# First stage of a two-layer kernel: GpSimd's fills behind the normalizations, the lambda chain ahead of the rows, weights split as q, k, v

## The chip, the cores and the metric

The kernel runs on one core of a Trainium2 chip. The metric is the device time of one execution in microseconds, from three timed runs of the kernel before; the median counts. The profile is of one execution, taken on its own.

## The reference

Two layers are computed, each an attention followed by a feed-forward part, each part added to the running rows `x`. Only the first attention is touched, and of it only the part up to q, k and v:

```python
def _layernorm(x, axis=-1, eps=1e-05):
    return (x - mean(x)) / sqrt(var(x) + eps)

x = L0_attn_x                       # (2, 1024, 256) float32
h = _layernorm(x)
qkv = h @ W_attn                    # (256, 768): q1, k1, q2, k2 (128 columns each), v (256)
lam = exp(dot(lambda_q1, lambda_k1)) - exp(dot(lambda_q2, lambda_k2)) + LAMBDA_INIT
attn1 = einsum('bthd,bshd->bhts', q1, k1) * scale
attn2 = einsum('bthd,bshd->bhts', q2, k2) * scale
score = softmax(attn1 - lam * attn2)          # 16 heads, hd = 8
out = (1 - LAMBDA_INIT) * einsum('bhts,bshd->bthd', score, v)
x = x + out @ W_proj
```

After it come a feed-forward part with ternary weights that keeps the largest tenth of its hidden units, a linear attention with 32 heads and a routed feed-forward part.

## The kernel before

The kernel is written as stages, each a block of five engine programs that wait for each other on semaphores only; a stage ends at a barrier of all engines, after which SyncE (SP) clears its semaphores. The order of each engine's work is written out by hand. The first stage is `stage_qkv` (line 158).

The 2048 rows are worked off in four chunks of 512 (`d.NC` = 4), each four tiles of 128 rows (`d.TPC`), with E = 256 as two halves of 128 (`d.KT` = 2). The rows stay in the tensor `residual` (X). For each chunk c:

- VectorE: `normal(c)` takes the statistics of the four tiles (lines 110, 113, 115: the variance plus epsilon), waits for ScalarE's root (line 137, `norm_root`), refines its reciprocal (lines 121 to 125) and applies mean and scale (line 142, one TENSOR_SCALAR for each tile, into `xn`).
- TensorE: `turn(c)` (line 366) transposes the eight 128 x 128 blocks of `xn` into PSUM.
- Each value that goes into a product is split in a high part and a low part; `mm_split` (line 153) makes three products of them. ScalarE copies out the high part (`high`, line 324), VectorE subtracts it (`low`, line 268).
- TensorE: four groups of 6 products of 512 columns for q and k (`ps_q`), then `turn(c + 1)`, then two times 12 products of 256 columns for v (`ps_v`).
- ScalarE and VectorE split q and k again (line 345, and `low_qk`, lines 277 and 282), and SP writes both parts to a DRAM tensor, two transfers for each of the four groups. ScalarE copies v into `v_rows` (`vall`, line 354), 32 columns for each head, of which 16 are v.

When chunk 1 (the last of the first batch) has been written, SP loads the first stack of q and k back from DRAM, into `qst` and `kst` of ring place 0; the attention stage needs it at its start.

Once, before all this: GpSimd makes the identity, fills `v_rows` with zeros (line 244, 128 x 8192), its column 16 of each head with a constant (line 245), and rows of the three `kst` tensors with ones (line 249, six fills of 32 x 2048). The weights are split into `w_hi` (ScalarE, lines 331 and 332) and `w_lo` (VectorE, lines 297 and 298), for each half k all of q, k and v, behind the normalization of chunk 0. The four lambda vectors come as rows of one partition (line 218, SP's queue); VectorE multiplies and sums them (lines 290, 291), ScalarE takes exp (line 335; Exp and Sqrt lie in different activation tables, so each switch is an ACT_TABLE_LOAD), VectorE makes the row of scales of it (lines 302 to 306), and TensorE turns this row into a column (line 373), which VectorE copies to `qs`. The scale `qs` is needed when q leaves PSUM. TensorE's q and k products of chunk 0 stand behind the column and behind the last `w_lo`.

The kernel already uses products whose result nobody reads: line 660 in the attention stage, 128 x 512 in full precision.

Of the kernel before, what the change touches and what calls it, by code (L numbers as in the profile page):

```python
# [28 lines left out]
def as_f32(ap):  # L29
    return ap.bitcast(F32)  # L30
# [127 lines left out]
def stage_qkv(nc, d, io, keep, scratch):  # L158


    with ExitStack() as ctx:
# [15 lines left out]
        lam_in = xn[0:1, 1]  # L177
        lam_pr = st.sb("lam_pr", [1, 2, d.E])
# [12 lines left out]
        dots, exps, row_ok, col_ok, qs_ok = (st.sem(n) for n in ("dots", "exps", "row_ok", "col_ok", "qs_ok"))  # L191
# [3 lines left out]
        v_ps, v_ok, v_init, pad_ok = (st.sem(n) for n in ("v_ps", "v_ok", "v_init", "pad_ok"))  # L195
# [12 lines left out]
        with nc.Block() as block:  # L208
            @block.sync
            def _(sp):  # L210
                for c in range(d.NC):
                    sl = slice(c * d.TPC, (c + 1) * d.TPC)
                    sp.dma_start(X[:, sl, :], x_tiles[:, sl, :]).then_inc(x_in[c], 16)
                    if c == 0:
                        sp.dma_start(w_raw[:], io["L0_attn_W_attn"].rearrange("(k p) n -> p k n", p=P))\
                            .then_inc(w_in, 16)
                        for n, name in enumerate(("q1", "k1", "q2", "k2")):
                            sp.dma_start(lam_in[:, n, :],
                                         io["L0_attn_lambda_" + name].rearrange("(a e) -> a e", a=1))\
                                .then_inc(lam_s, 16)  # L220
                for c in range(d.NC):
# [7 lines left out]
                    if c == d.S // d.CH - 1:  # L229
                        sp.wait_ge(pad_ok, 2 * len(kst))  # L230
# [6 lines left out]
            def _(pool):  # L237
# [6 lines left out]
                link(nc.gpsimd.memset(vall[:], 0.0))  # L244
                nc.gpsimd.memset(vall[:, :, :, d.HD:d.HD + 1], 1.0 / (1.0 - LAMBDA_INIT)).then_inc(v_init, 1)
                pool.wait_ge(v_init, 1)
                for i in range(2 * len(kst)):
                    rows = slice(ROW2 * (i % 2) + 32, ROW2 * (i % 2) + 64)
                    nc.gpsimd.memset(as_f32(kst[i // 2][rows, :, :]), 1.0).then_inc(pad_ok, 1)
                    pool.wait_ge(pad_ok, i + 1)  # L250

            @block.vector
            def _(dve):
                link = chain(dve, dv)

                def normal(c):
                    dve.wait_ge(x_in[c], 16)
                    norm_stats(nc, dve, link, w[c % 2], [X[:, d.TPC * c + j, :] for j in range(d.TPC)], c // 2 + 1)
# [25 lines left out]

                nc.vector.memset(one[:], 1.0)
                link(nc.vector.memset(row[:], 1.0))
                normal(0)

                dve.wait_ge(lam_s, 64)
                link(nc.vector.tensor_tensor(lam_pr[:], lam_in[:, 0::2, :], lam_in[:, 1::2, :], ALU.mult))  # L290
                nc.vector.reduce_sum(lam[0:1, 0:2], lam_pr[:], AX.X).then_inc(dots, 1)
                for k in range(d.KT):
                    dve.wait_ge(w_hi_ok, k + 1)
                    for part in range(2):
                        src, hi, lo = halves(k, part)
                        for a in range(2):
                            nc.vector.tensor_tensor(lo[:, :, a], src[:, :, a], as_f32(hi)[:, :, a], ALU.subtract)
                    nc.vector.tensor_tensor(w_lo[:, k, 2 * d.E:], w_raw[:, k, 2 * d.E:], as_f32(w_hi[:, k, 2 * d.E:]),
                                            ALU.subtract).then_inc(w_lo_ok, 1)
                low(0)  # L300
                dve.wait_ge(exps, 1)
                link(nc.vector.tensor_tensor(lam[0:1, 4:5], lam[0:1, 2:3], lam[0:1, 3:4], ALU.subtract))
                link(nc.vector.tensor_scalar(lam[0:1, 5:6], lam[0:1, 4:5], LAMBDA_INIT, -scale, ALU.add, ALU.mult))
                r = row[0:1, :].rearrange("p (h a e) -> p a h e", a=2, e=HD2)
# [5 lines left out]
                for c in range(d.NC):  # L310
                    if c + 1 < d.NC:
                        normal(c + 1)
# [2190 lines left out]
```

## Time and profile before

| what | value |
|---|---|
| median of three runs | 1221.81 us (1221.64 to 1226.63) |
| span of the profiled execution | 1222.5 us, 0.7 above the median |
| TensorE (PE) busy in the span | 1090.1 us (89%) |
| VectorE (DVE) busy | 916.0 us (75%) |
| ScalarE (ACT) busy | 623.8 us (51%) |
| GpSimd (POOL) busy | 218.6 us (18%) |
| end of the first stage (first instruction of the second) | 64.20 us |

The trace names each instruction by engine, line of the kernel, operation, output and inputs, with start and duration. PEld is TensorE's weight load, which overlaps products. A row "x4" is four instructions merged, and its duration runs from the first start to the last end. What stands in brackets is the idle time of the engine before the instruction, and who ended it. The names carry the stage: `qkv_xn` is `xn`, `residual` is X, `att_out` holds the high parts of q and k.

### The profile page before, as it was taken

Reading aid. Unit: us, or ns where it says so; the run is one execution under the profiler, and the core shown is the slowest. Engines: PE = TensorE matmul, PEld = TensorE weight load, DVE = VectorE, ACT = ScalarE, POOL = GpSimd, SP = SyncE. Lnnn points to the kernel's source line nnn. Section 1 sums busy time; section 2 is a strip of 40 time slices with the busy share of each in tenths; the row PEclk is TensorE's granted clock in tenths of the full one; section 3 lists DMA queues with packets and bytes.
Section 4 is the critical chain, followed back from the end, with each engine's and each line's share of the span. In section 5 each row is a group of like instructions: output and inputs, shape, how many; then the busy total and the mean of one; then the engine's idle time right before and its main releaser. Section 6 shows DMA issues by size and latency. Waiting matters only on the chain. (4 is left out here: it accounts for less than half of the span.)

```text
span 1222.5 us, 18399 instructions
## 1 busy us (share of the span) xinstructions
PE 1090.1 (89%) x7034; PEld 752.9 (62%) x7034; DVE 916.0 (75%) x1702; ACT 623.8 (51%) x1092; POOL 218.6 (18%) x173
## 2 busy tenths in 40 slices
PE   2969999999999998877877989999996999999978
PEld 2823333333333346666666768888885889899866
DVE  7778999999999824488898886555553878897832
ACT  2525878878788763766641233333334333433323
POOL 6004500000000001000034203000001744744300
PEclk9959999999999999888988989999997899999989
DMA  2880232143030000000000021011001000000010
GB/s 95 198 258 18 37 54 39 16 54 53 2 54 2 2 1 31 1 1 0 1 18 1 1 91 35 18 35 35 18 1 61 2 1 1 1 1 1 1 66 5
DMA packets 24850, 40.02 MB, mean 33 GB/s; under 512 B 3116, under 2 KB 12344, under 8 KB 24760
## 3 DMA queue, kind: packets, MB, share of 16 engines
q1 hardware_dynamic: 24760, 38.82, 13.7%
q8 instruction: 56, 0.92, 0.3%
q14 instruction: 34, 0.28, 0.1%
HBM read 28.06 MB, written 10.49 MB: 32 GB/s over the span
## 5 line engine op out<-in xcount | busy, mean ns | idle before, releaser
L721 DVE TENSOR_REDUCE att_mx<-att_ps_m 128x2 f32<-128x1024 f32 x256 | 310.9, 1225 | 25.1 <-PE att_ps_m L587 21.5
L698 ACT ACTIVATE att_prob<-att_ps_s 128x512 f32<-128x512 f32 x512 | 278.2, 596 | 89.9 <-PE att_ps_s L637 77.9
L653 PE MATMUL att_ps_o<-att_prob,v_rows 128*32 128x256 f32 (+1 forms) x1920 | 159.4, 405 | 0.0
L1931 POOL TENSOR_TENSOR qry_prod<-qry_qr,lin_ksum 128x512 f32<-128x512 f32 x64 | 92.9, 1452 | 303.0 <-ACT qry_qr L2052 288.9
L637 PE MATMUL att_ps_s<-qst,kst 50*128 50x512 f32 x512 | 128.0, 496 | 11.0 <-ACT att_prob L698 10.4
L637 PEld LDWEIGHTS att_ps_s<-qst,kst 50*128 50x128 f32 x512 | 48.1, 183 | 123.7 <-ACT att_prob L698 114.2
L587 PE MATMUL att_ps_m<-kst,qst 48*128 48x512 f32 x512 | 110.6, 427 | 9.0 <-DVE att_mx L721 6.9
L2052 ACT ACTIVATE qry_qr<-qry_ps_q 128x512 f32<-128x512 f32 x64 | 38.3, 598 | 132.9 <-PE qry_ps_q L153 124.0
L153 PE MATMUL qry_ps_o<-qry_m,qry_n_hi 128*128 128x256 f32 x512 | 99.7, 293 | 0.4 <-DVE qry_n_lo L1961 0.3
L1642 DVE SCALAR_TENSOR_TENSOR key_k_lo<-kf_ps,key_k_hi 128x512 fp32r<-128x512 f32 x64 | 44.2, 691 | 61.6 <-ACT key_k_hi L1720 61.0
L653 PEld LDWEIGHTS att_ps_o<-att_prob,v_rows 128*32 128x32 f32 x1920 | 38.1, 108 | 84.7 <-ACT att_prob L698 71.1
L153 PEld LDWEIGHTS qry_ps_o<-qry_m,qry_n_hi 128*128 128x128 f32 x512 | 78.6, 191 | 1.3 <-issue 0.7
L153 PE MATMUL qry_ps_o<-qry_m,qry_n_lo 128*128 128x256 f32 x256 | 71.8, 281 | 0.0
L1720 ACT ACTIVATE key_k_hi<-kf_ps 128x512 fp32r<-128x512 f32 x64 | 38.1, 597 | 64.3 <-PE kf_ps L153 57.1
L587 PEld LDWEIGHTS att_ps_m<-kst,qst 48*128 48x128 f32 x512 | 50.8, 194 | 23.5 <-DVE att_mx L721 19.8
L1961 DVE TENSOR_TENSOR qry_n_lo<-qry_ps_t,qry_n_hi 128x512 fp32r<-128x512 f32 x64 | 44.3, 692 | 23.2 <-ACT qry_n_hi L2041 21.4
L1951 DVE SCALAR_TENSOR_TENSOR qry_qn<-qry_rec,qry_qr 128x512 f32<-128x512 f32 x64 | 56.3, 880 | 2.2
L915 POOL MEMSET mlp_ones<- 128x128 f32 x1 | 0.2, 209 | 322.9 <-POOLq L525 322.9
L1946 DVE TENSOR_REDUCE qry_nrm<-qry_prod 128x8 f32<-128x512 f32 x64 | 43.7, 683 | 9.1 <-POOL qry_prod L1931 7.0
L153 PE MATMUL kf_ps<-key_k_hi,kf_xk 128*128 128x512 f32 x128 | 46.5, 404 | 4.6 <-DVE key_k_lo L1642 4.6
L153 PE MATMUL qry_ps_q<-qry_w_hi,kf_xt 128*128 128x512 f32 x128 | 47.4, 414 | 3.3 <-DVE qry_w_lo L2010 3.3
L153 PEld LDWEIGHTS qry_ps_o<-qry_m,qry_n_lo 128*128 128x128 f32 x256 | 48.9, 191 | 0.0
(425 smaller groups left out, 2336.8 us busy)
## 6 DMA issues: line engine op xcount, KB each, us to landing
qst<-qk_parts SPq DMA_DIRECT2D x48, 128.0 KB, 4.7
kst<-qk_parts SPq DMA_DIRECT2D x48, 128.0 KB, 7.3
qk_parts<-att_out SPq DMA_DIRECT2D x16, 256.0 KB, 5.6
qk_parts<-qk_lo SPq DMA_DIRECT2D x16, 256.0 KB, 5.8
residual<-L_attn_x SPq DMA_DIRECT2D x4, 512.0 KB, 6.1
lin_wq_raw<-L_attn_Wv SPq DMA_DIRECT2D x4, 512.0 KB, 3.7
lin_wq_raw<-L_attn_Wq SPq DMA_DIRECT2D x4, 512.0 KB, 5.3
lin_wq_raw<-L_attn_Wo SPq DMA_DIRECT2D x4, 512.0 KB, 3.9
```

The costliest lines, as they stand in the source:

```text
L153: ins = nc.tensor.matmul(out, a, b, start=first and n == 0, stop=last and n == len(terms) - 1)
L587: ins = nc.tensor.matmul(ps_m[:, n % 2, r, :], qst[g % RING][rows, v % NB, j, t * P:(t + 1) * P], kst[g % RING][rows, j, half * d.CH:(half ...
L637: ins = nc.tensor.matmul(ps_s[:, (n + r) % BANKS, :], kst[g % RING][rows, j, s * P:(s + 1) * P], qst[g % RING][rows, t, j, :], start=True, ...
L653: ins = nc.tensor.matmul(ps_o[32 * h:32 * h + 32, cols], vall[:, NS * b + s, h0 + h, :], prob[:, u % PR, h, cols], start=s == 0, stop=s == ...
L698: nc.scalar.activation(prob[:, u % PR, 2 * j + r, :], ps_s[:, (n + r) % BANKS, :], ACT.Exp).then_inc(exp_ok, 1)
L721: nc.vector.reduce_max(mx[:, v % 2, :, m], ps_m[:, n % 2], AX.X).then_inc(m_rd, 1)
L1642: nc.vector.scalar_tensor_tensor(out=k_lo[:, i % 2, :], in0=ps_k[:, i % 2, :], scalar=0.0, in1=as_f32(k_hi[:, i % 2, :]), op0=ALU.max, op1 ...
L1931: nc.gpsimd.tensor_tensor(prod[:, u % 2, :], qr[:, u % 2, :], ksum[:, b, cols(n)], ALU.mult).then_inc(pr_ok, 1)
L1946: link(nc.vector.tensor_reduce(nrm[:], prod[:, u % 2, :].rearrange("p (h e) -> p h e", e=HW), AX.X, ALU.add))
L1951: nc.vector.scalar_tensor_tensor(out=qn[:, u % 2, :].rearrange("p (h e) -> p h e", e=HW), in0=rec[:].unsqueeze(2).to_broadcast([P, HPB, HW ...
L1961: nc.vector.tensor_tensor(n_lo[:, u % 2, :], ps_t[:, u % 2, :], as_f32(n_hi[:, u % 2, :]), ALU.subtract).then_inc(n_ok, 1)
L2052: nc.scalar.activation(qr[:, u % 2, :], ps_q[:, u % 2, :], ACT.Relu).then_inc(q_ok, 1)
```

## The change

GpSimd. Of its fills only the two of `kst` 0 stay in front; then it does the scalar tail of lambda (two operations on one element and one on 64), waits until all four chunks are normalized, and does the other fills: column 16 of each head, the columns behind it (15 of 32, where before it zeroed all 32), and `kst` 1 and 2. SP's wait ahead of the first stack load is for `kst` 0 alone. ScalarE's wait for the fill of `v_rows` goes.

Lambda. The four vectors are loaded by ScalarE's queue, as 128 partitions x 2 elements each. TensorE makes the two dots as four products of one column, ScalarE takes exp of them straight from PSUM, ahead of its first root. The row of scales is prepared by VectorE as constants.

Weights. Split part by part (0: q of both kinds, 1: k, 2: v) rather than half by half; TensorE's q products wait for part 0, its k products for part 1, v for part 2, and each half k of chunk 0 for its own `xt_lo`. VectorE does low_w(0), low(0), low_w(1), the statistics of chunk 1, low_w(2), and then waits for the column.

TensorE. Unread products of 128 columns: six after the identity, sixteen after the dots, four after the column. In chunk 0 the order is q and k, first half of v, `turn(1)`, second half of v.

The diff, with unchanged lines mostly left out and eight spaces of indentation removed:

```diff
 qk_hi = keep["AO"][:].bitcast(F32R).rearrange("p (c j a) e -> p c j (a e)", c=2, j=NQ)
-lam_in = xn[0:1, 1]
-lam_pr = st.sb("lam_pr", [1, 2, d.E])
+lam_in = st.sb("lam_in", [P, 4, d.KT])
 lam = st.sb("lam", [1, 8])
...
 dv, gp, w_hi_ok, w_lo_ok = st.sem("dv"), st.sem("gp"), st.sem("w_hi_ok"), st.sem("w_lo_ok")
-dots, exps, row_ok, col_ok, qs_ok = (st.sem(n) for n in ("dots", "exps", "row_ok", "col_ok", "qs_ok"))
+dots, exps, row_1, row_ok, col_ok, qs_ok = (
+    st.sem(n) for n in ("dots", "exps", "row_1", "row_ok", "col_ok", "qs_ok"))
+WARM = 16
 xn_ok, xt_ps, hi_ok, lo_ok = (st.sem(n) for n in ("xn_ok", "xt_ps", "hi_ok", "lo_ok"))
...
 qk_out = scratch["qk_out"]
-v_ps, v_ok, v_init, pad_ok = (st.sem(n) for n in ("v_ps", "v_ok", "v_init", "pad_ok"))
+v_ps, v_ok, pad_ok = (st.sem(n) for n in ("v_ps", "v_ok", "pad_ok"))
 id_ok, stack_in = st.sem("id_ok"), st.sem("stack_in")
...
                     .then_inc(w_in, 16)
-                for n, name in enumerate(("q1", "k1", "q2", "k2")):
-                    sp.dma_start(lam_in[:, n, :],
-                                 io["L0_attn_lambda_" + name].rearrange("(a e) -> a e", a=1))\
-                        .then_inc(lam_s, 16)
         for c in range(d.NC):
...
             if c == d.S // d.CH - 1:
-                sp.wait_ge(pad_ok, 2 * len(kst))
+                sp.wait_ge(pad_ok, 2)
                 for i in range(d.S // d.CH):
...
-        link(nc.gpsimd.memset(vall[:], 0.0))
-        nc.gpsimd.memset(vall[:, :, :, d.HD:d.HD + 1], 1.0 / (1.0 - LAMBDA_INIT)).then_inc(v_init, 1)
-        pool.wait_ge(v_init, 1)
-        for i in range(2 * len(kst)):
-            rows = slice(ROW2 * (i % 2) + 32, ROW2 * (i % 2) + 64)
-            nc.gpsimd.memset(as_f32(kst[i // 2][rows, :, :]), 1.0).then_inc(pad_ok, 1)
-            pool.wait_ge(pad_ok, i + 1)
+        def pads(i):
+            for r in range(2):
+                rows = slice(ROW2 * r + 32, ROW2 * r + 64)
+                nc.gpsimd.memset(as_f32(kst[i][rows, :, :]), 1.0).then_inc(pad_ok, 1)
+                pool.wait_ge(pad_ok, 2 * i + r + 1)
+        pads(0)
+        pool.wait_ge(exps, 1)
+        link(nc.gpsimd.tensor_tensor(lam[0:1, 4:5], lam[0:1, 2:3], lam[0:1, 3:4], ALU.subtract))
+        link(nc.gpsimd.tensor_scalar(lam[0:1, 5:6], lam[0:1, 4:5], LAMBDA_INIT, -scale, ALU.add, ALU.mult))
+        pool.wait_ge(row_1, 1)
+        r = row[0:1, :].rearrange("p (h a e) -> p a h e", a=2, e=HD2)
+        nc.gpsimd.tensor_scalar(r[:, 1], r[:, 1], lam[0:1, 5:6], None, ALU.mult).then_inc(row_ok, 1)
+        pool.wait_ge(xn_ok, d.NC)
+        link(nc.gpsimd.memset(vall[:, :, :, d.HD:d.HD + 1], 1.0 / (1.0 - LAMBDA_INIT)))
+        link(nc.gpsimd.memset(vall[:, :, :, d.HD + 1:], 0.0))
+        for i in range(1, len(kst)):
+            pads(i)
...
+        def var(c):
+            dve.wait_ge(x_in[c], 16)
+            norm_var(nc, link, w[c % 2], [X[:, d.TPC * c + j, :] for j in range(d.TPC)])
         def normal(c):
-            dve.wait_ge(x_in[c], 16)
-            norm_stats(nc, dve, link, w[c % 2], [X[:, d.TPC * c + j, :] for j in range(d.TPC)], c // 2 + 1)
+            norm_rstd(nc, dve, link, w[c % 2], c // 2 + 1)
             if c >= 2:
...
+        def low_w(part):
+            for k in range(d.KT):
+                dve.wait_ge(w_hi_ok, d.KT * part + k + 1)
+                if part == 2:
+                    ins = nc.vector.tensor_tensor(w_lo[:, k, 2 * d.E:], w_raw[:, k, 2 * d.E:],
+                                                  as_f32(w_hi[:, k, 2 * d.E:]), ALU.subtract)
+                else:
+                    src, hi, lo = halves(k, part)
+                    for a in range(2):
+                        ins = nc.vector.tensor_tensor(lo[:, :, a], src[:, :, a], as_f32(hi)[:, :, a],
+                                                      ALU.subtract)
+            ins.then_inc(w_lo_ok, 1)
         nc.vector.memset(one[:], 1.0)
-        link(nc.vector.memset(row[:], 1.0))
+        r = row[0:1, :].rearrange("p (h a e) -> p a h e", a=2, e=HD2)
+        nc.vector.memset(r[:, 1], 1.0)
+        nc.vector.memset(r[:, 0], scale).then_inc(row_1, 1)
+        var(0)
         normal(0)
-        dve.wait_ge(lam_s, 64)
-        link(nc.vector.tensor_tensor(lam_pr[:], lam_in[:, 0::2, :], lam_in[:, 1::2, :], ALU.mult))
-        nc.vector.reduce_sum(lam[0:1, 0:2], lam_pr[:], AX.X).then_inc(dots, 1)
-        for k in range(d.KT):
-            dve.wait_ge(w_hi_ok, k + 1)
-            for part in range(2):
-                src, hi, lo = halves(k, part)
-                for a in range(2):
-                    nc.vector.tensor_tensor(lo[:, :, a], src[:, :, a], as_f32(hi)[:, :, a], ALU.subtract)
-            nc.vector.tensor_tensor(w_lo[:, k, 2 * d.E:], w_raw[:, k, 2 * d.E:], as_f32(w_hi[:, k, 2 * d.E:]),
-                                    ALU.subtract).then_inc(w_lo_ok, 1)
+        low_w(0)
         low(0)
-        dve.wait_ge(exps, 1)
-        link(nc.vector.tensor_tensor(lam[0:1, 4:5], lam[0:1, 2:3], lam[0:1, 3:4], ALU.subtract))
-        link(nc.vector.tensor_scalar(lam[0:1, 5:6], lam[0:1, 4:5], LAMBDA_INIT, -scale, ALU.add, ALU.mult))
-        r = row[0:1, :].rearrange("p (h a e) -> p a h e", a=2, e=HD2)
-        nc.vector.tensor_scalar(r[:, 1], r[:, 1], lam[0:1, 5:6], None, ALU.mult)
-        nc.vector.tensor_scalar(r[:, 0], r[:, 0], scale, None, ALU.mult).then_inc(row_ok, 1)
+        low_w(1)
+        var(1)
+        low_w(2)
         dve.wait_ge(col_ok, 1)
         nc.vector.tensor_copy(qs[:, 0:1], ps_v[:, 0, 0, 0:1]).then_inc(qs_ok, 1)
-        dve.wait_ge(qs_ok, 1)
         for c in range(d.NC):
             if c + 1 < d.NC:
+                if c:
+                    var(c + 1)
                 normal(c + 1)
+            if c == 0:
+                dve.wait_ge(qs_ok, 1)
             low_qk(c)
...
+        def high_w(part):
+            for k in range(d.KT):
+                if part == 2:
+                    ins = nc.scalar.activation(w_hi[:, k, 2 * d.E:], w_raw[:, k, 2 * d.E:], ACT.Copy)
+                else:
+                    src, hi, _ = halves(k, part)
+                    ins = nc.scalar.activation(hi, src, ACT.Copy)
+                ins.then_inc(w_hi_ok, 1)
+        for n, name in enumerate(("q1", "k1", "q2", "k2")):
+            nc.scalar.dma_start(lam_in[:, n, :], io["L0_attn_lambda_" + name].rearrange("(p k) -> p k", p=P))\
+                .then_inc(lam_s, 16)
+        act.wait_ge(dots, 1)
+        nc.scalar.activation(lam[0:1, 2:4], ps_v[0:1, 1, 1, 0:2], ACT.Exp).then_inc(exps, 1)
         norm_root(nc, act, w[0], 1)
         act.wait_ge(w_in, 16)
-        for k in range(d.KT):
-            for part in range(2):
-                src, hi, _ = halves(k, part)
-                nc.scalar.activation(hi, src, ACT.Copy)
-            nc.scalar.activation(w_hi[:, k, 2 * d.E:], w_raw[:, k, 2 * d.E:], ACT.Copy).then_inc(w_hi_ok, 1)
+        for part in range(3):
+            high_w(part)
         high(0)
-        act.wait_ge(dots, 1)
-        nc.scalar.activation(lam[0:1, 2:4], lam[0:1, 0:2], ACT.Exp).then_inc(exps, 1)
         for c in range(d.NC):
...
                 act.wait_ge(v_ps, 2 * c + j + 1)
-                if c == 0:
-                    act.wait_ge(v_init, 1)
                 t = d.TPC * c + 2 * j
...
+        def keep_busy(n):
+            for _ in range(n):
+                nc.tensor.matmul(ps_q[:, NQ - 1, 0:P], ident[:], ident[:], start=True, stop=True)
+        def values(c, j):
+            if c == 0:
+                pe.wait_ge(qs_ok, 1)
+                pe.wait_ge(w_lo_ok, 3)
+            else:
+                pe.wait_ge(v_ok, 2 * (c - 1) + j + 1)
+            for i in range(2):
+                t = slice((2 * j + i) * P, (2 * j + i + 1) * P)
+                for k in range(d.KT):
+                    ins = mm_split(nc, ps_v[:, j, i, :], xt_hi[:, c % 2, k, t], xt_lo[:, c % 2, k, t],
+                                   w_hi[:, k, 2 * d.E:], w_lo[:, k, 2 * d.E:], k == 0, k == d.KT - 1)
+            ins.then_inc(v_ps, 1)
         pe.wait_ge(id_ok, 1)
+        keep_busy(6)
+        pe.wait_ge(lam_s, 64)
+        for n in range(2):
+            for k in range(d.KT):
+                ins = nc.tensor.matmul(ps_v[0:1, 1, 1, n:n + 1], lam_in[:, 2 * n, k:k + 1],
+                                       lam_in[:, 2 * n + 1, k:k + 1], start=k == 0, stop=k == d.KT - 1)
+        ins.then_inc(dots, 1)
+        keep_busy(WARM)
         turn(0)
...
             .then_inc(col_ok, 1)
-        pe.wait_ge(w_lo_ok, d.KT)
+        keep_busy(4)
         for c in range(d.NC):
-            pe.wait_ge(lo_ok, d.KT * (c + 1))
             for j in range(NQ):
...
                     pe.wait_ge(qk_lo_ok, NQ * (c - 1) + j + 1)
+                elif j % 2 == 0:
+                    pe.wait_ge(w_lo_ok, j // 2 + 1)
                 for k in range(d.KT):
+                    if j == 0:
+                        pe.wait_ge(lo_ok, d.KT * c + k + 1)
                     cols = slice(j * P, (j + 1) * P)
...
                 ins.then_inc(qk_ps, 1)
+            if c == 0:
+                values(c, 0)
+                turn(c + 1)
+                values(c, 1)
+                continue
             if c + 1 < d.NC:
...
             for j in range(2):
-                if c == 0:
-                    pe.wait_ge(qs_ok, 1)
-                else:
-                    pe.wait_ge(v_ok, 2 * (c - 1) + j + 1)
-                for i in range(2):
-                    t = slice((2 * j + i) * P, (2 * j + i + 1) * P)
-                    for k in range(d.KT):
-                        ins = mm_split(nc, ps_v[:, j, i, :], xt_hi[:, c % 2, k, t], xt_lo[:, c % 2, k, t],
-                                       w_hi[:, k, 2 * d.E:], w_lo[:, k, 2 * d.E:], k == 0, k == d.KT - 1)
-                ins.then_inc(v_ps, 1)
+                values(c, j)
 st.clear()
```

## Rows read from the trace of the kernel before

**Rows 1.** The page's first line: span and number of instructions.

```profile
span 1222.5 us, 18399 instructions
```

**Rows 2.** Stretches (us, busy and count by engine, PEclk, DMA share, GB/s).

```profile
0.00:24.54 24.54, 2.45 (x10) 2.06 (x10) 18.26 (x38) 7.29 (x13) 19.09 (x14) 1.00 0.37 118
...
35.46:44.80 9.34, 9.34 (x60) 8.33 (x59) 8.10 (x26) 4.95 (x9) 0.00 (x0) 1.00 0.59 218
```

**Rows 3.** Timeline, 0 to 20 us, all engines (start, us, engine, line, work, [idle <-releaser]).

```profile
1.53 6.92 POOL L244 MEMSET v_rows<- 128x8192 f32 x1
...
5.32 1.41 DVE L110 BATCH_NORM_STATS2 qkv_stats<-residual 128x6 f32<-128x256 f32 x4 [4.30 <-DMA residual<-L_attn_x]
...
8.51 0.53 POOL L245 MEMSET v_rows<- 128x256 f32 x1
...
8.62 0.71 ACT L331 ACTIVATE qkv_w_hi<-qkv_w_raw 128x256 fp32r<-128x256 f32 x2
...
9.10 11.22 POOL L249 MEMSET kst<- 32x2048 f32 x6
...
11.16 7.42 DVE L142 TENSOR_SCALAR qkv_xn<-residual,qkv_mv,qkv_rstd 128x256 f32<-128x256 f32 x4
...
18.50 0.67 DVE L290 TENSOR_TENSOR qkv_lam_pr<-qkv_xn 1x512 f32<-1x512 f32 x1
```

**Rows 4.** Single lines, 0 to 60 us (duration ns min/median/max, first and last start).

```profile
L142 DVE TENSOR_SCALAR qkv_xn<-residual,qkv_mv,qkv_rstd x16: 404/410/1972, 11.2 to 47.9; 128x256 f32<-128x256 f32 x16
...
L115 DVE TENSOR_SCALAR qkv_ve<-qkv_mv x4: 170/170/1301, 7.2 to 45.5; 128x4 f32<-128x4 f32 x4
...
L124 DVE TENSOR_SCALAR qkv_t<-qkv_t x4: 170/170/1572, 9.4 to 46.6; 128x4 f32<-128x4 f32 x4
```

**Rows 5.** Timeline, 20 to 36.6 us.

```profile
20.95 0.88 DVE L297 TENSOR_TENSOR qkv_w_lo<-qkv_w_raw,qkv_w_hi 128x128 fp32r<-128x128 f32 x4
...
22.83 1.28 ACT L137 ACT_TABLE_LOAD   x1
...
24.03 0.58 PE L373 MATMUL qkv_ps_v<-qkv_one,qkv_row 1*128 1x1 f32 x2 [3.37 <-DVE qkv_row L306]
...
24.84 1.41 DVE L110 BATCH_NORM_STATS2 qkv_stats<-residual 128x6 f32<-128x256 f32 x4
...
25.13 0.63 PE L153 MATMUL qkv_ps_q<-qkv_xt_lo,qkv_w_hi 128*128 128x512 f32 x1
...
27.14 0.18 DVE L121 RECIPROCAL qkv_r<-qkv_sd 128x4 f32<-128x4 f32 x1 [0.27 <-ACT qkv_sd L137]
...
28.12 0.45 PE L153 MATMUL qkv_ps_q<-qkv_xt_hi,qkv_w_lo 128*128 128x512 f32 x1
...
28.15 1.38 DVE L142 TENSOR_SCALAR qkv_xn<-residual,qkv_mv,qkv_rstd 128x256 f32<-128x256 f32 x4
...
29.45 1.41 DVE L277 SCALAR_TENSOR_TENSOR qk_lo<-qkv_ps_q,qkv_qs,att_out 128x512 fp32r<-128x512 f32 x2
...
31.82 1.03 PE L366 MATMUL qkv_ps_t<-ident,qkv_xn 128*128 128x128 f32 x8
...
33.25 1.28 DVE L268 TENSOR_TENSOR qkv_xt_lo<-qkv_ps_t,qkv_xt_hi 128x512 fp32r<-128x512 f32 x2
...
35.56 0.40 PE L153 MATMUL qkv_ps_q<-qkv_xt_hi,qkv_w_hi 128*128 128x512 f32 x1
...
35.79 0.40 PE L153 MATMUL qkv_ps_q<-qkv_xt_lo,qkv_w_hi 128*128 128x512 f32 x1
```

**Rows 6.** Timeline of TensorE, second stage, unread products (line 660).

```profile
86.47 2.07 PE L660 MATMUL att_ps_s<-v_rows,att_ones 128*128 128x512 f32 x2
...
93.96 1.12 PE L660 MATMUL att_ps_s<-v_rows,att_ones 128*128 128x512 f32 x2
```

**Rows 7.** Timeline of ScalarE, end of the first stage.

```profile
62.54 0.60 ACT L354 ACTIVATE v_rows<-qkv_ps_v 128x512 f32<-128x512 f32 x1 [0.84 <-PE qkv_ps_v L153]
```

**Rows 8.** DMA queues, 6 to 10 us (packets, MB, share of 16 engines).

```profile
q1 hardware_dynamic: 1345, 1.44, 107.6%
```

## The prediction

> **What bounds the kernel now.** I read the page first. One core runs stages that follow each other behind barriers, over a span of 1222.5 us [rows 1]; that profiled execution is 0.7 us above the median of the timed runs, 1221.8, so a saving read from the trace is taken off the median unchanged. The change touches the first stage alone, so the question is how much earlier the second stage can begin. The table of stretches [rows 2] says where to look. In the first 24.54 us TensorE is busy for 2.45 us and VectorE for 18.26: this is a start-up chain. In a steady chunk (35.46 to 44.80) TensorE is busy throughout and VectorE for 8.10 of 9.34 us: TensorE sets the pace there. The change can gain in the start-up and cannot shorten a steady chunk. I measure everything by one mark, the first product of chunk 1, at 35.56 [rows 5]; after it the stage is the same code, apart from GpSimd's fills.
>
> **What the start-up waits for.** The timeline [rows 3] shows VectorE sitting until the first rows land at 5.32. The normalization of chunk 0 then ends at 18.58. Chunk 1 does the same work from 24.84 to 29.53, in 4.7 us [rows 5]. The groups by line say where the difference lies: the apply (L142) has a median of 0.410 us and a maximum of 1.972, and two four-element operations (L115, L124) have 0.170 and maxima of 1.301 and 1.572 [rows 4]. These long ones all stand beside GpSimd's fills (v_rows from 1.53, kst from 9.10, six in 11.22 us, so 1.87 us each), and the four applies end about where fills end: 7.42 us for four is one per fill of 1.87. The excess is 1.13 + 1.40 + 6.04 = 8.6 us. Not every VectorE operation suffers: the statistics beside the fills take 1.41 us for four, as they do alone in chunk 1, and a TENSOR_TENSOR at 18.50 runs inside a fill in 0.67 us, for 512 elements of one partition. So what is slow is TENSOR_SCALAR from SBUF to SBUF beside a GpSimd fill.
>
> **The change, part by part.**
>
> *GpSimd's fills.* Only the two fills of kst 0 stay in front (2 x 1.87 from about 1.5, over at about 5.3, when the rows land). VectorE's TENSOR_SCALARs then run clear of fills: -8.6 us on the path. The rest goes behind the last normalization, whose last apply starts at 47.9 and ends at 48.3 in the old clock [rows 4]: 0.53 for the strided ones, 15/32 of 6.92 = 3.2 for the zeros, 4 x 1.87 = 7.5, in all 11.3, so to 59.6, when ScalarE's last copy starts at 62.54 and ends at 63.1 [rows 7]. Nothing waits inside: 0 on the path. If the zeros cost per element what the strided fill does (0.53 / 256 = 2.07 ns, 3840 elements, 7.9 us) it ends at 64.3, 1.2 us late; 0 to 1.2, I take 0, since only a fixed cost in the short fill need explain its rate. Beside these fills VectorE runs subtractions out of PSUM. No row has such a subtraction beside a fill; the nearest is the TENSOR_TENSOR at 18.50, which was not held up. If each of them had to wait for the fill that runs, like the applies, the first would lose up to 3.2 - 0.7 = 2.5 us and the next two 1.87 - 0.7 = 1.2 each, 4.9 in all ahead of chunk 3's products, less the 1 us by which VectorE leads TensorE (34.53 against 35.56); bounds 0 to 3.9, I take 0.
>
> The Trainium skill ("SBUF — State Buffer", section "SBUF: two separate sides") says that VectorE and GpSimd share a port pair as an exclusive lock for a whole instruction, against VectorE operations in a two-port mode or, where GpSimd reads SBUF, with two SBUF inputs. By that rule a fill would leave a subtraction from PSUM alone, and the loss at the end would be 0. No row here shows that pair.
>
> *The four lambda loads.* They leave SP's queue, are issued by ScalarE, and become 128 partitions x 2 elements each: 512 packets of 8 bytes where there were four rows of 1 KB. No row prices an 8-byte packet. In the busiest stretch of the row loads, 1345 packets took 107.6% of 16 engines for 4 us, 51 ns each, nearly all of them 1 KB [rows 8]. Below: 0 (they move in the gaps before the rows come). Above: 32 packets per engine x 51 ns = 1.6 us, added to the first rows. I take 0.8: rows at 6.1. Lambda is taken to land with them at 6.1.
>
> The Trainium skill ("DMA: Bandwidth & Descriptors", section "Specifications") puts full rate at 512 bytes or more and says that smaller transfers are done as read-modify-write. That speaks against this edit; what it would do if it were expensive is the third rival.
>
> *The lambda chain.* It was TENSOR_TENSOR, a reduction, an Exp between two table loads (1.28 each [rows 5]), four small VectorE operations, a product and a copy, with the qkv products standing behind it. Now the dots are products on TensorE (0.6 us for a product with its second pass, [rows 5], so 6.1 to 6.7), Exp 0.2, and the table load for Sqrt 1.3: ScalarE is ready for the root at about 8.3. The variance is ready at 6.1 + 2.0 = 8.1. So the root comes 0.2 late, and the rows are normalized at 6.1 + 4.7 + 0.2 = 11.0, where it was 18.6. GpSimd takes the scalar tail in its idle time. Behind Exp on ScalarE stand the root, six weight copies (two in 0.71, so 2.1 us, to about 10.7 [rows 3]) and the copy of the turned rows, which comes later.
>
> *Unread products.* Six before lambda, sixteen after it, four after the turn. They stand in TensorE's queue ahead of the turn. A full-precision product appears as two records, 2.07 us for 512 columns while TensorE ran at the lower of its two levels (1.2 GHz) and 1.12 at the upper (2.4) [rows 6]; a quarter, for 128 columns, is 0.52 and 0.28. From 6.7, sixteen take 4.5 us (to 11.2) or 8.3 (to 15.0). In the start-up the granted clock is printed as 1.00 [rows 2], yet the durations tell of the lower level first: TensorE was at work from 24.03 to 28.12, and then its products fell from 0.63 to 0.45 us and less [rows 5]. By that, eight at 0.52 and eight at 0.28 end at 13.1; if the clock has risen sooner, after the six early ones, sooner. I take the turn at 12.0, between 11.2 and 13.1, so the unread products hold the turn up by about 1 us over the normalized rows. It was at 18.73. What they give back (eight qkv products at 0.63 instead of 0.40) is not on the path that follows.
>
> *Weights split as q, k, v.* From the turn T to the end of low(0): 2.7 us (31.82 to 34.53 in chunk 1). low_w(0) is done by 11.9, so it hides behind ScalarE's copy. Then VectorE carries low_w(1), four TENSOR_TENSORs, 0.9; var(1), 2.0 (24.84 to the end of L115; the reciprocal follows at 27.14, after the root); low_w(2), as many columns as low_w(1) in half the instructions, 0.8; the copy of qs 0.2; the rest of the normalization of chunk 1, 27.14 to 29.53, 2.4; low_qk(0), 4 x 0.7 = 2.8; the first half of low(1), 0.65. Sum 9.75. So chunk 1's first product is at T + 12.45. Is TensorE ready? Turn, one product and four unread ones end at T + 2.4, 24 products started 0.23 apart (35.56 to 35.79) at T + 7.9, the first half of the values, 1.4 (a chunk of 9.3 less 5.5 and the turn's 1.0, halved), at T + 9.3; the second turn waits for normalized rows until T + 9.1, so it ends, 1.0 later and with a little for the handover, at T + 10.4, and the second half of the values at T + 11.8. VectorE decides by 0.6 us. If eight of the 24 products last 0.63 instead of 0.40, as the first ones did here, TensorE is the later one, by 1.2 us.
>
> *Sum.* 12.0 + 12.45 = 24.45 against 35.56: 11.1 us. Of that 6.7 is the earlier turn (8.6 of fills, less what the lambda loads and unread products cost), and 4.4 the shorter way from turn to chunk 1.
>
> *Afterwards.* VectorE now starts on chunk 2's rows 0.65 us after TensorE's mark, where it led by 1.0 us (34.53 against 35.56). It needs 2.3 + 2.4 + 2.8 + 0.65 = 8.15 us to the next low half, so it is there 8.8 us after the mark, against a TensorE chunk of 9.3: in time, with 0.5 to spare. SP's writes to DRAM and the stack loads hang on chunks 0 and 1 and move along. So 1221.8 - 11.1 = 1210.7.
>
> **The rivals.**
>
> 1. *Unread products end early.* The turn goes with the normalized rows, undelayed by small packets: T = 10.0 to 11.2, saving 13.1 to 11.9: 1208.7 to 1209.9. For it: only 0.28 each at 2.4 GHz. Chance 0.2.
>
> 2. *They stay at 1.2 GHz, or lambda is late.* T = 13.1 to 15.0, saving 10.0 to 8.1: 1211.8 to 1213.7. For it: the first eight qkv products of the profile, all at the lower level. Chance 0.17.
>
> 3. *Slower: 8-byte packets.* Lambda gates Exp, Exp the root, and the root everything. T = landing + 5.0 by the root or + 6.8 by the unread products. The saving is 23.1 - T, so it is gone with a landing at 16.3 and turns into +0.5% (6.1 us) at 22.4. That takes 0.64 us per packet instead of 0.051, giving 1228. Nothing in the rows excludes it outright. Chance 0.03.
>
> 4. *Given back.* VectorE's lost lead makes each of three chunks wait: 1.5 us each plus a hold by the late fills of 3.9 leaves 11.1 - 8.4 = 2.7: 1219.1. Against it: 8.10 busy of 9.34. Chance 0.06.
>
> 5. *Only the late fills cost*, 1.2 to 3.9: 1211.9 to 1214.6. Chance 0.06.
>
> **How the numbers follow.** My forecast (T from 11.2 to 13.1, 1209.9 to 1211.8) has 0.48. I give 1210.7 and the range 1208.3 to 1214.6, which takes in rivals 1, 2 and 5 with 0.4 us of spread of the runs; 0.09 and some unknown stay outside. 0.5% (6.1 us) is about what this kernel's measurement can tell from no change. Faster by more: 0.48 + 0.2 + 0.17 + 0.06 = 0.91. Within: 0.06. Slower: 0.03.
>
> **What would show it.** The four applies of chunk 0 take 1.4 us, and L115 and L124 0.17. The rows land at 5.3 to 6.9. The first turn stands at 11.2 to 13.1 with TensorE at work right up to it; if a gap stands ahead of it, the normalized rows decide. Chunk 1's first product comes at about 24.5, released by VectorE's low(1), and the later chunks keep 9.2 to 9.4 us. GpSimd's last fill ends about 3 us before the stage does; subtractions beside it keep 0.69. The second stage keeps its length. Wrong would be: a root that waits long for Exp, a fill at the barrier, or later stages whose lengths change by microseconds.

## The result and the profile after

The kernel after runs in 1213.01 us (median of four, 1212.19 to 1216.01) against 1223.14 for the kernel before on the same chip (1221.64 to 1226.63). The ratio is 0.9929 with a 95% interval of 0.9908 to 0.9949: 8.7 us faster, between 6.2 and 11.2. The prediction said 11.1 us faster, 1208.3 to 1214.6. The direction and the range held. The sum was 2.4 us above the measured 8.7; the timed runs alone don't show this, as 11.1 lies inside their interval, but the trace does, with 8.35 us at the end of the stage.

The timeline of the kernel after, 0 to 17 us, all engines:

```profile
1.53 2.93 PE L396 MATMUL qkv_ps_q<-ident 128*128 128x128 f32 x12 [1.53 <-POOL ident L237]
1.53 3.65 POOL L244 MEMSET kst<- 32x2048 f32 x2
...
5.03 1.41 DVE L110 BATCH_NORM_STATS2 qkv_stats<-residual 128x6 f32<-128x256 f32 x4 [4.00 <-DMA residual<-L_attn_x]
...
8.39 0.34 PE L416 MATMUL qkv_ps_v<-qkv_lam_in 128*1 128x1 f32 x8 [3.93 <-DMA qkv_lam_in<-L_attn_lambda_k]
...
8.66 6.35 PE L396 MATMUL qkv_ps_q<-ident 128*128 128x128 f32 x32
8.76 0.16 ACT L355 ACTIVATE qkv_lam<-qkv_ps_v 1x2 f32<-1x2 f32 x1 [4.83 <-PE qkv_ps_v L416]
8.94 1.28 ACT L137 ACT_TABLE_LOAD   x1
...
10.24 0.21 ACT L137 ACTIVATE qkv_sd<-qkv_ve 128x4 f32<-128x4 f32 x1
...
10.47 0.18 DVE L121 RECIPROCAL qkv_r<-qkv_sd 128x4 f32<-128x4 f32 x1 [3.42 <-ACT qkv_sd L137]
...
11.48 1.38 DVE L142 TENSOR_SCALAR qkv_xn<-residual,qkv_mv,qkv_rstd 128x256 f32<-128x256 f32 x4
...
14.84 1.04 PE L389 MATMUL qkv_ps_t<-ident,qkv_xn 128*128 128x128 f32 x8
```

Against [rows 3]: the applies take 1.38 us where they took 7.42. The rows land at 5.03, no later than before. But VectorE's reciprocal waits 3.42 us for ScalarE's root, the root stands behind the table load, that behind Exp, and Exp behind lambda, for which TensorE waited until 8.39. The rows are normalized at 12.86. The turn comes 2 us later still, behind the unread products that end at about 14.8. Both waits are what the change itself put there.

The two lines that tell of GpSimd's fills, single lines of the kernel after (duration ns min/median/max), where [rows 4] had maxima of 1972 and 1301:

```profile
L142 DVE TENSOR_SCALAR qkv_xn<-residual,qkv_mv,qkv_rstd x16: 405/408/414, 11.5 to 39.4; 128x256 f32<-128x256 f32 x16
L115 DVE TENSOR_SCALAR qkv_ve<-qkv_mv x4: 170/171/171, 6.9 to 36.9; 128x4 f32<-128x4 f32 x4
```

The timeline of TensorE gives the marks: chunk 1's first product at 26.42 (35.56 in [rows 5]) and chunk 2's at 35.71. The end of the stage, from the timelines of VectorE, GpSimd, ScalarE and SP's queue:

```profile
39.69 1.41 DVE L288 SCALAR_TENSOR_TENSOR qk_lo<-qkv_ps_q,qkv_qs,att_out 128x512 fp32r<-128x512 f32 x2
39.84 0.60 POOL L255 MEMSET v_rows<- 128x256 f32 x1 [29.77 <-DVE qkv_xn L142]
...
40.50 3.33 POOL L256 MEMSET v_rows<- 128x3840 f32 x1
41.01 0.68 DVE L293 TENSOR_TENSOR qk_lo<-qkv_ps_q,att_out 128x512 fp32r<-128x512 f32 x1
...
43.88 7.38 POOL L244 MEMSET kst<- 32x2048 f32 x4
...
53.47 0.60 ACT L377 ACTIVATE v_rows<-qkv_ps_v 128x512 f32<-128x512 f32 x1 [0.84 <-PE qkv_ps_v L153]
...
54.55 0.46 SPq L224 DMA_DIRECT2D qk_parts<-qk_lo  x1
...
55.85 0.21 POOL L603 MEMSET att_ones<- 128x128 f32 x1 [4.59 <-POOLq L75]
```

GpSimd's fills end at 51.3, 3.7 us ahead of SP's last issue. The subtractions out of PSUM beside them take 0.68, and 1.41 for two, as alone: the hold that the prediction bounded with 3.9 us isn't there. ScalarE is done at 54.07 but SP still issues writes, the last until 55.01, and the second stage starts 0.84 us after that. So the second stage starts 8.35 us sooner (64.20 to 55.85), and not the 9.14 of the mark.

### The profile page after: what moved, and what is told of

Its sections match the earlier page's. It is cut to its first block and busy times, and to the rows that moved or that the text cites. A ratio compares the mean times of both kernels' runs of the same rounds, so it can differ in the third digit from the quotient of the medians.

```text
span 1211.0 us, 18514 instructions
## 1 busy us (share of the span) xinstructions
PE 1093.7 (90%) x7094; PEld 757.6 (63%) x7094; DVE 904.9 (75%) x1697; ACT 621.9 (51%) x1091; POOL 215.8 (18%) x176
```

## The experiments

Each is compared by three times of its own profile: the first turn T, the first product of chunk 1 (the mark), and the start of the second stage; and by the ratio of its time to the kernel before, timed in the same rounds. The kernel before has two profiles, and its mark differs by 0.74 us between them (last row), so a difference of that size at the mark shows nothing.

| kernel | T | mark | second stage | ratio (95%) |
|---|---|---|---|---|
| before | 18.73 | 35.56 | 64.20 | 1 |
| after | 14.84 | 26.42 | 55.85 | 0.9929 (0.9908 to 0.9949) |
| e_fills | 10.16 | 27.19 | 55.7 | 0.9931 (0.9911 to 0.9952) |
| e_nofills | 17.43 | 32.03 | 63.6 | 0.9971 (0.9956 to 0.9987) |
| e_warm0 | 13.26 | 26.93 | 56.5 | 0.9951 (0.9934 to 0.9967) |
| e_root | 13.93 | 25.51 | 54.6 | one run, 1214.51 us |
| e_root_warm0 | 9.92 | 24.30 | 53.9 | 0.9928 (0.9911 to 0.9946) |
| e_rows | 12.41 | 23.99 | 54.0 | one run, 1213.6 us |
| e_merge | 14.26 | 25.84 | 54.5 | 0.9928 (0.9902 to 0.9954) |
| e_best | 9.87 | 22.11 | 50.8 | 0.9880 (0.9858 to 0.9902) |
| e_best_narrow | 9.90 | 23.40 | 53.1 | 0.9882 (0.9865 to 0.9898) |
| e_before_again | 18.73 | 36.30 | 64.5 | one run, 1221.56 us |

**One part alone: the fills.** The kernel before, with only this (and SP's wait for two of the pads, and no v_init):

```diff
-link(nc.gpsimd.memset(vall[:], 0.0))
-nc.gpsimd.memset(vall[:, :, :, d.HD:d.HD + 1], ...)
-for i in range(2 * len(kst)): ...
...
+pads(0)
+pool.wait_ge(xn_ok, d.NC)
+link(nc.gpsimd.memset(vall[:, :, :, d.HD:d.HD + 1], 1.0 / (1.0 - LAMBDA_INIT)))
+link(nc.gpsimd.memset(vall[:, :, :, d.HD + 1:], 0.0))
+for i in range(1, len(kst)):
+    pads(i)
```

> The kernel before with one part of the change: GpSimd's fills moved (only kst 0 in front, the rest behind the fourth normalization). Theory (the fills are the gain): the four applies of chunk 0 take 1.4 us instead of 7.4, the first turn stands at about 10.1 instead of 18.7, the first product of chunk 1 at 35.56 - 8.6 = 27.0, which is within 0.6 us of the full change (26.42), so the time is 8 to 9 us below before and about that of the full change. Rival (lambda, the split of the weights and the unread products carry a third, 4.4 - 0 us as the prediction had it): chunk 1 at 27.0 all the same but at least 3 us of time above the full change.

The first theory held: T 8.57 us sooner, mark 8.37 sooner, and a time that can't be told from that of the full change (0.9931 and 0.9929). Timeline of e_fills:

```profile
8.63 1.38 DVE L142 TENSOR_SCALAR qkv_xn<-residual,qkv_mv,qkv_rstd 128x256 f32<-128x256 f32 x4
...
10.16 1.94 PE L369 MATMUL qkv_ps_t<-ident,qkv_xn 128*128 128x128 f32 x8 [10.16 <-DVE qkv_xn L142]
...
15.47 0.58 PE L376 MATMUL qkv_ps_v<-qkv_one,qkv_row 1*128 1x1 f32 x2 [3.38 <-DVE qkv_row L311]
```

The turn is 4.7 us earlier than in the full change, and 5.3 us then go by before the column: the lambda chain and the weights between turn and products, which the full change removes. All other parts together win 0.8 us at the mark, about the mark's own spread, and nothing at the second stage (55.7 and 55.85).

**All but the fills.** The full change with every fill in front of lambda's tail.

```diff
-pads(0)
+link(nc.gpsimd.memset(vall[:, :, :, d.HD:d.HD + 1], 1.0 / (1.0 - LAMBDA_INIT)))
+link(nc.gpsimd.memset(vall[:, :, :, d.HD + 1:], 0.0))
+for i in range(len(kst)):
+    pads(i)
 pool.wait_ge(exps, 1)
```

> The full change with all of GpSimd's fills back in front (lambda's scalar tail behind them). Theory: the applies of chunk 0 wait for fills again, GpSimd is busy until about 16.5 us and the row of scales comes after it; the first turn goes back to 17 to 19 us and chunk 1 to 29 to 31, so the time is 3 to 5 us above the full change and 5 to 6 below before. Rival (the port matters little once the chain is reordered): chunk 1 at 27 or sooner.

Timeline of VectorE in e_nofills:

```profile
11.41 1.46 DVE L124 TENSOR_SCALAR qkv_t<-qkv_t 128x4 f32<-128x4 f32 x1
...
13.11 4.27 DVE L142 TENSOR_SCALAR qkv_xn<-residual,qkv_mv,qkv_rstd 128x256 f32<-128x256 f32 x4
```

The applies take 4.27 us and L124 1.46 beside the fills; T is 17.43. The mark came at 32.03, 1 us later than expected. The time is about 5 us above the full change, as expected, and 3.5 us below the kernel before, where 5 to 6 were expected. So with the fills in front the other parts are worth 3.5 us, and with the fills moved nothing that the time shows: the two gains don't add up. The second stage's 63.6 says little here: the profiled execution took 1222.93 us, against a median of 1217.72 over twelve, and in it SP issued until 62.76, 3.2 us after ScalarE's last copy, with most of its last sixteen writes at 0.5 to 0.7 us, where the full change has 0.4 to 0.5.

**Without the sixteen unread products.**

```diff
 ins.then_inc(dots, 1)
-keep_busy(WARM)
 turn(0)
```

> The full change without the sixteen unread products after the dots. Theory (they hold the turn): the first turn goes with the normalized rows at 12.9 instead of 14.84, so chunk 1 comes up to 2 us sooner, 24.5 to 25.5, less what a lower clock costs the first qkv products. Rival (they pay for themselves by the clock): the first qkv products take 0.63 instead of 0.40 us and chunk 1 comes no sooner than 26.4.

Timeline of TensorE in e_warm0:

```profile
13.26 1.97 PE L389 MATMUL qkv_ps_t<-ident,qkv_xn 128*128 128x128 f32 x8 [4.19 <-DVE qkv_xn L142]
...
15.67 2.08 PE L396 MATMUL qkv_ps_q<-ident 128*128 128x128 f32 x8
```

T is 1.6 us earlier, but the turn takes 1.97 instead of 1.04 and the four unread products 2.08 instead of 1.16: TensorE is at its lower level there, and the mark is 0.5 us later. The rival held in its size but not in its place: of the 24 qkv products only the first is longer than before (0.68), and the price was paid ahead of them. Where they stand, the sixteen cost a delay and buy back as much. The ratio, 0.9951, is above that of the full change, but the intervals overlap.

**The root ahead of Exp, alone.**

```diff
+norm_root(nc, act, w[0], 1)
 act.wait_ge(dots, 1)
 nc.scalar.activation(lam[0:1, 2:4], ps_v[0:1, 1, 1, 0:2], ACT.Exp).then_inc(exps, 1)
-norm_root(nc, act, w[0], 1)
```

> The full change with ScalarE's first root ahead of Exp and nothing else. Theory (two holds, and the unread products are the outer one): the rows are normalized at 9.8 instead of 12.9, but the sixteen unread products end at 14.8 as before, so the turn and chunk 1 stay within 0.3 us of the full change (14.84, 26.42). Rival (the late root was the hold): the turn at 13 or sooner and chunk 1 at 25 or sooner.

Timeline of VectorE in e_root:

```profile
8.30 1.38 DVE L142 TENSOR_SCALAR qkv_xn<-residual,qkv_mv,qkv_rstd 128x256 f32<-128x256 f32 x4
```

The applies start at 8.30 and end at 9.68, 3.2 us sooner, and the turn still waits for the unread products. They took 5.34 us here (6.35 in the full change), so T and the mark are 0.9 sooner than in the full change, outside the 0.3 expected. The sixteen took 5.3 to 6.4 us in five profiles with the same code: TensorE's level rose 3.5 us after the first of them here and 5.5 us after it in the full change (from 4 or 5 records in half a microsecond to 7).

**Both at once**: the edits of e_root and e_warm0 together.

> As e_warm0, and ScalarE takes its first root ahead of lambda's Exp. Theory (two holds in a row: lambda's landing at 8.39 holds Exp and so the root, the unread products hold the turn): the rows are normalized at 9.7, the turn stands at 9.8, the high parts wait for the weight copies until about 11, and chunk 1 comes at 22.5 to 24.0: 2.5 to 4 us below the full change. Rival (lambda's landing decides anyway, by the scales or by the weight copies behind Exp): chunk 1 at 25 or later, time within 1.5 us of the full change.

T is 9.92 as expected. The mark, 24.30, is 0.3 later than the range: the turn takes 1.97 us again, and the first qkv products after their first take 0.63 us. The stage is 2.0 us shorter than in the full change, less than the 2.5 expected, and in the time (0.9928) nothing of it can be told.

**Lambda as rows.** Loaded as four rows of 1 KB. The dots wait for the rows but read a constant tile, which VectorE fills, so this kernel leaves lambda's value out.

```diff
-nc.scalar.dma_start(lam_in[:, n, :], io["L0_attn_lambda_" + name].rearrange("(p k) -> p k", p=P))
+nc.scalar.dma_start(lam_row[:, n, :], io["L0_attn_lambda_" + name].rearrange("(a e) -> a e", a=1))
```

> The full change with lambda loaded as four rows of 1 KB (4 packets) from ScalarE's queue instead of 512 packets of 8 bytes; the dots read a tile of constants but still wait for the loads, so lambda's value is left out of the computation. Theory (the small packets make lambda late): the dots run by 5.0 to 6.0 instead of 8.39, the root no longer waits (7.1 instead of 10.24), the rows are normalized at 9.7, and the turn follows the unread products, 12 to 12.6. Rival (lambda waits behind the rows and the weights in the DMA engines, whatever its packets): the dots still at 7.5 to 8.5.

Timeline of e_rows, then DMA queues, 0 to 12 us, of the kernel after (packets, MB, share of 16 engines):

```profile
6.43 0.34 PE L418 MATMUL qkv_ps_v<-qkv_lam_in 128*1 128x1 f32 x8 [1.98 <-DMA qkv_lam_row<-L_attn_lambda_k]
...
8.28 0.21 ACT L137 ACTIVATE qkv_sd<-qkv_ve 128x4 f32<-128x4 f32 x1
...
12.41 1.04 PE L391 MATMUL qkv_ps_t<-ident,qkv_xn 128*128 128x128 f32 x8
```

```profile
q1 hardware_dynamic: 2384, 2.88, 70.8%
q10 hardware_dynamic: 576, 0.00, 2.6%
```

The dots run 2.0 us sooner, not the 2.4 to 3.4 expected, and the root still waits (8.28, not 7.1), for Exp and its table load. T is where it was expected. So the form of the load is worth 2 us, and it isn't the engines' time: 576 packets in 2.6% of 16 engines for 12 us are 9 ns each. They land late: the dots start 6.2 us after the last of the four issues, and 4.6 us after it with rows of 1 KB. VectorE starts on the rows at 4.90 here and at 5.03 in the full change, so the small packets hardly delay them. Why they land late isn't shown.

**SP's wide writes.** For chunks 2 and 3 one transfer takes two groups.

```diff
+wide = 2 if c >= d.S // d.CH else 1
-for j in range(NQ):
+for j in range(0, NQ, wide):
-    sp.wait_ge(qk_lo_ok, NQ * c + j + 1)
+    sp.wait_ge(qk_lo_ok, NQ * c + j + wide)
```

> The full change, and SP writes q and k of chunks 2 and 3 with one transfer for two groups instead of one for each (8 issues fewer). In the full change SP's last issue ends at 55.01, 0.94 us after ScalarE's last copy (54.07), and the second stage starts 0.84 after it. Theory (SP's queue ends the stage there): SP is done ahead of ScalarE, the first product of chunk 1 stays at 26.4, and the second stage starts at about 55.0 instead of 55.85. Rival (the barrier waits for ScalarE or for the landing of the stack): the second stage still starts 29.4 us after that product. In the time, 0.85 us is at the edge of what can be told.

The second stage starts 28.65 us after the mark instead of 29.43: 0.8 of the 0.85 expected. SP's last issue still ends after ScalarE's last copy, at 53.67 against 53.49. The mark itself was 0.6 sooner, by shorter unread products (5.62 us). The time doesn't resolve it (0.9928).

**A version made of these findings**: e_root, eighteen unread products ahead of the dots and none behind them, wide writes.

```diff
 pe.wait_ge(id_ok, 1)
-keep_busy(6)
+keep_busy(18)
 pe.wait_ge(lam_s, 64)
...
-keep_busy(WARM)
```

> The full change with ScalarE's first root ahead of Exp, eighteen unread products ahead of the dots in place of six and none of the sixteen behind them, and SP's wide writes of e_merge. Theory: TensorE reaches the upper clock while it waits for lambda (products of 0.49 us each until about 5.5, then 0.26, over at 8.5), the turn stands at 9.9 and takes 1.04, the first qkv product comes at 12.4, chunk 1 at 22.0 to 22.5, the second stage at 50.8 to 51.5, 4.4 to 5 us ahead of the full change; time about 1208.5. Rival (SP's queue or the write of chunk 1 takes the gain away): chunk 1 at 22.0 to 22.5 but the second stage not before 53.

Timeline of e_best:

```profile
1.53 6.88 PE L398 MATMUL qkv_ps_q<-ident 128*128 128x128 f32 x36 [1.53 <-POOL ident L239]
...
8.91 0.34 PE L418 MATMUL qkv_ps_v<-qkv_lam_in 128*1 128x1 f32 x8 [0.50 <-DMA qkv_lam_in<-L_attn_lambda_k]
...
9.87 1.09 PE L391 MATMUL qkv_ps_t<-ident,qkv_xn 128*128 128x128 f32 x8 [0.63 <-DVE qkv_xn L142]
```

The unread products now lie in time in which TensorE waited anyway, and the turn runs at the upper level (1.09) straight behind the normalized rows. Mark and second stage are as expected. By its ratio, 0.9880 (1207.65 us), it is 14.7 us faster than before, between 12 and 17, and its interval lies wholly below that of the full change. The stage is 13.4 us shorter.

**The same with narrow writes**: e_best with SP's loop as it was.

> As e_best, but SP writes q and k of chunks 2 and 3 with one transfer for each group again. Theory (SP's queue ends the stage once TensorE is early): the first product of chunk 1 stays at 22.1 (within 0.7), but the second stage starts 29.7 to 30.5 after it, 52.0 or later, against 28.7 in e_best. Rival (TensorE and ScalarE end the stage): the second stage starts 28.7 after it, at 50.8.

Timelines of TensorE and of ScalarE and GpSimd in e_best_narrow:

```profile
8.55 0.34 PE L416 MATMUL qkv_ps_v<-qkv_lam_in 128*1 128x1 f32 x8 [1.16 <-DMA qkv_lam_in<-L_attn_lambda_k]
9.90 1.09 PE L389 MATMUL qkv_ps_t<-ident,qkv_xn 128*128 128x128 f32 x8 [1.01 <-DVE qkv_xn L142]
...
11.59 2.01 PE L396 MATMUL qkv_ps_q<-ident 128*128 128x128 f32 x8
...
13.83 0.63 PE L153 MATMUL qkv_ps_q<-qkv_xt_lo,qkv_w_hi 128*128 128x512 f32 x1
...
50.37 0.60 ACT L377 ACTIVATE v_rows<-qkv_ps_v 128x512 f32<-128x512 f32 x1 [0.84 <-PE qkv_ps_v L153]
...
53.10 0.21 POOL L602 MEMSET att_ones<- 128x128 f32 x1 [5.05 <-POOLq L75]
```

The second stage starts 29.7 us after the mark, as SP's queue would have it, against 28.7. The mark missed its 22.1 by 1.3 us: TensorE had idled 1.16 and 1.01 us around the dots (0.50 and 0.63 in e_best), and by the four unread products after the column (2.01 us) it was back at the lower level. TensorE's code is the same in both kernels, so this is a difference between two executions, and e_best's mark is the better of the two; how often it comes isn't known. In its time the kernel is as fast as e_best (0.9882), so the wide writes show in the trace, as the 1.0 us between mark and second stage, and not in the time.

**The kernel before, profiled again.**

> The kernel before, unchanged, profiled a second time. In the profiles so far the time from the start of the second stage to the last transfer lies between 1150.8 and 1157.6 us, with the same code behind that start. Theory (it varies from execution to execution): for the kernel before it differs from its first profile (1156.2) by 1 us or more, while the first stage repeats within 0.3 us (second stage at 64.2). Rival (the later stages depend on what the first stage does): it repeats 1156.2 within 0.5 us.

The mark and the second stage's first instruction in this second profile, from the timelines of TensorE and GpSimd:

```profile
36.30 0.40 PE L153 MATMUL qkv_ps_q<-qkv_xt_hi,qkv_w_hi 128*128 128x512 f32 x1
...
64.54 0.21 POOL L555 MEMSET att_ones<- 128x128 f32 x1 [44.21 <-POOLq L75]
```

From the second stage's start to the last transfer's issue it took 1153.1 us, against 1156.2 in the first profile, with the second stage at 64.5: the first theory, with 0.3 us in the first stage. Inside the first stage it doesn't repeat as well: T is 18.73 in both, but here eleven of the first qkv products last 0.6 us or more, against eight in the first profile, and the mark is 0.74 us later. Over all twelve profiles the time from the second stage's start to the last issue lies between 1150.8 and 1157.6. A difference of 3 us between two spans need therefore be no effect of the first stage; the 11.5 us between the two spans (1222.5 and 1211.0) are 8.35 of the change and 3.15 of such scatter.

## Why the prediction was right, and where it was off

*The fills.* Right, with its size: 8.6 us on VectorE, 8.57 at the turn of e_fills. The fills behind the fourth normalization cost nothing (0 taken, up to 3.9 bounded): GpSimd needs 11.4 us for them and has 15. By the lock rule of the Trainium skill ("SBUF — State Buffer", section "SBUF: two separate sides") a fill leaves a VectorE subtraction out of PSUM alone, and the trace agrees, with 0.68 us at 41.01.

*The four lambda loads.* Wrong in both directions. They were said to delay the rows to 6.1 and to land with them. The rows came at 5.03 (nothing taken away), lambda at 8.39. The price was looked for in the engines' time, where it is 9 ns for each packet, and it was in the landing, 2.0 us by e_rows. No run shows the 0.8 us that the prediction took for the rows' delay. The page "DMA: Bandwidth & Descriptors" (the Trainium skill, section "Specifications"), with its warning of transfers below 512 bytes, pointed the right way; no run shows whether read-modify-write is the reason.

*The lambda chain.* Here the root was said to be 0.2 us late; it was 3.2 late. The mechanism was named, the landing was its missing term. A root that waits long for Exp was one of the prediction's own signs of being wrong, and it came.

*The unread products.* T was to be 12.0 and was 14.84. Of the 2.84, 2.0 come from where they start (8.66 for 6.7) and the rest from their length (6.35 for the 5.3 that T = 12.0 meant; the bounds 4.5 and 8.3 held). The forecast's own band for T, 11.2 to 13.1 with a chance of 0.48, was missed; the second rival happened, near its late end (13.1 to 15.0, chance 0.17). That they hold the turn over the normalized rows was forecast, with 1 us; it was 2.0. What they give back was put off the path, and this step failed: without them (e_warm0) the turn is 1.6 us sooner, but from turn to mark it takes 13.67 us instead of 11.58, of which 0.93 are the turn and 0.92 the four unread products at the lower level. So removing them alone gains nothing.

*From turn to chunk 1.* T + 12.45 was forecast, T + 11.58 measured. VectorE's sum counted durations end to end, but neighbours overlap by 0.08 us or so and low_w(2) took 0.75. That gave 0.9 us back. VectorE seems to decide the mark, as forecast, but by 0.1 us or so: TensorE's last product for v starts 0.20 us ahead of it, where 0.12 is the usual distance, and VectorE's first low half of chunk 1 is over at about 26.3 (two in 1.28 from 25.59). The trace names no wait there.

*Afterwards.* This step failed: VectorE is "in time" for TensorE, but SP's writes don't "move along". VectorE starts chunk 2's rows later than TensorE's mark, so low_qk(1) and the first write of chunk 1 come 5.74 us after the mark, against 4.25 in the kernel before and in e_fills. On that write hangs the stack load, on this the writes of chunks 2 and 3, 16 us of issuing in SP's queue almost without a pause, and on their end the barrier. SP's queue in the kernel before, then in the kernel after:

```profile
39.81 0.32 SPq L227 DMA_DIRECT2D qk_parts<-att_out  x1
...
62.78 0.58 SPq L227 DMA_DIRECT2D qk_parts<-qk_lo  x1
```

```profile
32.16 0.32 SPq L224 DMA_DIRECT2D qk_parts<-att_out  x1
...
39.04 4.82 SPq L467 DMA_DIRECT2D qst<-qk_parts  x6
```

In the kernel before, too, SP's last issue ends after ScalarE's last copy (63.36 and 63.14), and the second stage starts 0.84 us after it; so the queue was at the limit already, which the prediction, with its eye on ScalarE's copy, didn't see. From its first write of chunk 1 SP needs 23.55 us there and 22.85 in the kernel after. That takes 0.7 of the 1.5 us back, and 0.8 of the mark's 9.14 are lost, shown by e_merge, which gets them back.

*The sum.* 11.1 forecast; 9.14 at the mark, 8.35 at the second stage, 8.7 (6.2 to 11.2) in the time. The terms account for it: 11.1 less 2.84 for the later turn, plus 0.87 on the way to chunk 1, less 0.79 at SP's queue. The turn is 3.9 us sooner where 6.7 were forecast, the way to chunk 1 5.25 us shorter where 4.4 were. The result lies in the range by the fills, whose 8.6 us were read rightly and which alone give this time (e_fills); the 2.5 us that the other parts were to add didn't come. It was luck in part that their errors, both ways, stayed within it.

## What to carry to other kernels

When one engine's fills hold another, moving the fills may be the whole gain; test it alone before counting the rest. When an engine's queue waits for a small load ahead of the critical step, that load's landing becomes critical: keep such a wait behind the step. Put work that nobody reads where the engine idles anyway, not between a result and its use. Look for what ends a stage, a queue that issues DMAs included, before taking the lead of a mark for a gain of time. And profile the same kernel twice before reading a difference of a few tenths of a microsecond.

## What the runs showed of the hardware

TENSOR_SCALARs of four elements, too, waited beside a fill (1.30 and 1.57 us for 0.17 in [rows 4]). A TENSOR_TENSOR of the same size, from SBUF to SBUF, didn't: in the kernel before L123 takes 0.16 us at 9.16, inside the fill that starts at 9.10. Nor did subtractions with an operand in PSUM (0.68 us). Small packets were cheap in the DMA engines (9 ns each) and late to land (6.2 us). The granted clock is printed as 1.00 in the first stretches even where the turn takes 1.94 us instead of 1.04, so there the durations are what tells TensorE's level. And the upper level can be lost again: in e_best_narrow the four unread products at 11.59 took 2.01 us instead of 1.16, after a turn at the upper level (1.09) and two waits of 1.2 and 1.0 us ahead of it; the granted clock of 11.00 to 15.00 is 0.59 there. That the waits caused it isn't shown.
